# Four cross-attention layers on one core: interleaved opening, and a mask split into eight pieces

## The reference

```python
def bit_quant(W):
    gamma = jnp.mean(jnp.abs(W))
    Wq = jnp.clip(jnp.round(W / (gamma + Q_EPS)), -1.0, 1.0) * gamma
    return W + jax.lax.stop_gradient(Wq - W)
...
xn = layer_norm(x, ln_gamma, ln_beta)
q = xn @ bit_quant(Wq).T + bq
k = context @ bit_quant(Wk).T + bk
v = context @ bit_quant(Wv).T + bv
```

```python
scores = jnp.einsum('bhqd,bhkd->bhqk', q, k) / math.sqrt(HD)
scores = scores + attention_mask
```

## Time and profile before

| | us |
|---|---|
| median of 3 runs | 585.86 |
| lowest, highest | 583.68, 589.11 |
| the profiled execution | 585.07 |
| its span, first to last instruction | 583.3 |

### The profile page before, as it was taken

One profiled execution on the slowest core, in us unless ns is written; L12 is line 12 of the kernel. 1 busy time (PEld: TensorE's weight loads), 2 busy tenths in 40 slices (PEclk: granted clock), 3 DMA queues, 4 the chain that ended last, 5 costly groups with the idle time before them and its releaser, 6 DMA issues.

```text
span 583.3 us, 14128 instructions
## 1 busy us (share of the span) xinstructions
PE 506.8 (87%) x5446; PEld 404.7 (69%) x5446; DVE 404.7 (69%) x1005; ACT 316.9 (54%) x761; POOL 251.8 (43%) x281
## 2 busy tenths in 40 slices
PE   0699999879999996895669699899999999998985
PEld 0367887657777775784547477788787878776874
DVE  4368866788777775256487979787878987784522
ACT  1177887647777776475242636455564636344331
POOL 4645633478788787889310313132222223112110
PEclk9999999989999999999678999999999999999998
DMA  9920000000000000000000000000000000000000
GB/s 295 269 111 3 2 3 3 2 3 1 3 4 2 3 3 1 1 1 2 0 1 0 2 1 0 1 1 11 2 10 1 1 11 1 9 2 10 1 10 18
DMA packets 12121, 11.75 MB, mean 20 GB/s; under 512 B 5144, under 2 KB 10136, under 8 KB 11928
## 3 DMA queue, kind: packets, MB, share of 16 engines
q1 hardware_dynamic: 11624, 9.54, 5.9%
q10 hardware_dynamic: 432, 1.32, 0.6%
HBM read 9.81 MB, written 1.05 MB: 19 GB/s over the span
## 4 chain that ended last, share of the span: by engine, by line
PE 51%; DVE 26%; issue 10%; POOL 7%; ACT 5%; DMA 1%; POOLq 0%; DVEq 0%; ACTq 0%
PE ps L436 7%; DVE wide L1225 5%; PE ps L450 4%; PE ps L426 4%; PE ps L418 4%; PE ps L574 4%; DVE wide L1230 3%; PE ps L588 3%; PE ps L610 3%; DVE mx L1286 2%; PE ps L664 2%; PE ps L379 2%; DVE p L1288 2%; PE ps L461 2%; PE ps L380 2%
## 5 line engine op out<-in xcount | busy, mean ns | idle before, releaser
L1446 POOL TENSOR_TENSOR probs<-p,rc 128x512 f32<-128x512 f32 x32 | 33.7, 1054 | 155.9 <-DVE rc L1297 155.9
L1057 DVE TENSOR_REDUCE negm<-ps 128x8 bf16<-128x512 f32 x96 | 59.6, 682 | 24.8 <-PE ps L418 24.8
L911 ACT ACTIVATE p<-p 128x512 f32<-128x512 f32 x32 | 20.2, 631 | 101.2 <-DVE p L1288 101.2
L574 PE MATMUL ps<-shared,wq 128*128 128x256 f32 x256 | 68.7, 396 | 4.6 <-DVE w L1256 2.3
L765 ACT ACTIVATE shared<-ps 128x512 f32<-128x512 f32 x96 | 57.4, 600 | 24.3 <-PE ps L436 22.6
L1408 POOL TENSOR_TENSOR wide<-wide,cv 128x1024 f32<-128x1024 f32 x24 | 49.3, 2053 | 48.4 <-DVE wide L1036 48.4
L1353 POOL TENSOR_TENSOR rstd<-veps,neghalf 128x2 f32<-128x2 f32 x40 | 29.1, 728 | 74.6 <-DVE veps L1081 47.5
L1225 DVE TENSOR_TENSOR wide<-ps,cst 128x512 f32<-128x512 f32 x64 | 43.2, 675 | 25.4 <-PE ps L574 25.4
L436 PE MATMUL ps<-cst,p 128*128 128x128 f32 x384 | 59.2, 278 | 0.4 <-ACT shared L765 0.4
L759 ACT ACTIVATE p<-ps 128x512 f32<-128x512 f32 x96 | 54.5, 596 | 7.4 <-PE ps L426 7.3
L574 PEld LDWEIGHTS ps<-shared,wq 128*128 128x128 f32 x256 | 46.6, 195 | 15.5 <-DVE w L1256 4.3
(11 more groups left out here) (180 smaller groups left out, 1173.3 us busy)
## 6 DMA issues: line engine op xcount, KB each, us to landing
late<-in_mask_l SPq DMA_DIRECT2D x2, 512.0 KB, 8.7
wq<-in_wq SPq DMA_DIRECT2D x1, 1024.0 KB, 8.6
result<-x_all SPq DMA_DIRECT2D x8, 128.0 KB, 1.8
x_all<-in_x_tok SPq DMA_DIRECT2D x1, 896.0 KB, 9.9
wide<-in_ctx_t SPq DMA_DIRECT2D x1, 896.0 KB, 11.6
rv<-in_rv ACTq DMA_DIRECT2D x1, 768.0 KB, 7.4
cst<-in_cst ACTq DMA_DIRECT2D x1, 512.0 KB, 4.8
wa<-in_wa SPq DMA_DIRECT2D x1, 512.0 KB, 9.5
```

The costliest lines, as they stand in the source:

```text
L574: ins = mm(bank_of(f"q{i}", g)[:, j * GT:j * GT + GT], wq3[:, 2 * i + j, :], hn_t[:, g % 2, 0:GT], start=True, stop=True, skip_group_check ...
L1057: V.tensor_reduce(negm[:, n % 4, :], ps[:, S_BANK[r], :].rearrange("p (a k) -> p a k", k=S), AX.X, ALU.max, negate=True).then_inc(sm["dve_ ...
```

## The change

In the opening, group 1 gets PSUM bank N for its input, q, k and v, so it needn't wait for v of group 0. The four matrices are quantised one by one, each with a semaphore count of its own; q and k need two, v three, and the output projection all four. The fourth is quantised in pass 0, behind two evacuations of v. Normalising group 1 moves from POOL to DVE (norm0). The first loads of x and of the context bring two groups. ACT first loads only the identity (64 KB) and the columns of biases, and issues the rest of its loads when the first part of the context is there; it casts the other selectors in pass 4. The mask is split in eight pieces of 256 columns in passes 10 to 17, all five operations of a piece in one pass.

```diff
-        A, N, PV = ps[:, A_BANK, :], ps[:, N_BANK, :], ps[:, PV_BANK, :]
+        N, PV = ps[:, N_BANK, :], ps[:, PV_BANK, :]
+
+        def a_bank(w):
+            return ps[:, N_BANK if w == 1 else A_BANK, :]
...
-            eng.dma_start(x_all[:, 0:TG, :], x_v[:, 0:TG, :]).then_inc(sm["ld_x0"], 16)
-            eng.dma_start(ctx_t[:, 0:GT], dr["ctx_t"][:, 0:GT]).then_inc(sm["ld_ctx0"], 16)
-            eng.dma_start(x_all[:, TG:NT, :], x_v[:, TG:NT, :]).then_inc(sm["ld_x"], 16)
-            eng.dma_start(ctx_t[:, GT:], dr["ctx_t"][:, GT:]).then_inc(sm["ld_ctx"], 16)
+            eng.dma_start(x_all[:, 0:2 * TG, :], x_v[:, 0:2 * TG, :]).then_inc(sm["ld_x0"], 16)
+            eng.dma_start(ctx_t[:, 0:2 * GT], dr["ctx_t"][:, 0:2 * GT]).then_inc(sm["ld_ctx0"], 16)
+            eng.dma_start(x_all[:, 2 * TG:NT, :], x_v[:, 2 * TG:NT, :]).then_inc(sm["ld_x"], 16)
+            eng.dma_start(ctx_t[:, 2 * GT:], dr["ctx_t"][:, 2 * GT:]).then_inc(sm["ld_ctx"], 16)
...
-                if w >= 1:
-                    pe.wait_ge(sm["dve_v"], w)
+                if w >= 2:
+                    pe.wait_ge(sm["dve_v"], 1 if w == 2 else w)
...
                 if w == 0:
-                    pe.wait_ge(sm["quant"], 1)
+                    pe.wait_ge(sm["quant"], 2)
...
             def project_v(w):
                 ph = w // NG
                 pe.wait_ge(sm["act_q"], w + 1)
+                if w == 0:
+                    pe.wait_ge(sm["quant"], 3)
...
             def project_out(w):
                 pe.wait_ge(sm["act_at"], w + 1)
+                if w == 0:
+                    pe.wait_ge(sm["quant"], 4)
...
             transposes_in(0)
             project_qk(0)
-            project_v(0)
             transposes_in(1)
             project_qk(1)
+            project_v(0)
...
-            pe.wait_ge(sm["m3_split"], 1)
+            pe.wait_ge(sm["m3_split"], 5 * (B // 4))
...
-            act.dma_start(cst[:, :], dr["cst"]).then_inc(sm["ld_small"], 16)
+            act.dma_start(cst[:, 0:128], dr["cst"][:, 0:128]).then_inc(sm["ld_small"], 16)
             act.dma_start(cv[:, :], dr["cv"]).then_inc(sm["ld_small"], 16)
+            act.wait_ge(sm["ld_small"], 32)
+            A_(idb[:, 0, :], cst[:, 0:128], ACT.Copy).then_inc(sm["cst_bf"], 1)
+            act.wait_ge(sm["ld_ctx0"], 16)
             act.dma_start(rv[:, :, :].rearrange("p a b -> p (a b)"), dr["rv"].partition_broadcast(128))\
                .then_inc(sm["ld_rv"], 16)
-            act.wait_ge(sm["ld_small"], 32)
-            A_(idb[:, :, :].rearrange("p a b -> p (a b)"), cst[:, 0:128 * NSEL], ACT.Copy).then_inc(sm["cst_bf"], 1)
+            act.dma_start(cst[:, 128:], dr["cst"][:, 128:]).then_inc(sm["ld_cst"], 16)
+
+            def cast_selectors():
+                act.wait_ge(sm["ld_cst"], 16)
+                A_(idb[:, 1:, :].rearrange("p a b -> p (a b)"), cst[:, 128:128 * NSEL], ACT.Copy).then_inc(sm["cst_bf"], 1)
...
             for w in range(NW + 2):
+                if w == 4:
+                    cast_selectors()
...
+            def quantise(i):
+                c = slice(i * 128, i * 128 + 128)
+                pos, neg, w = probs_t[:, 0, c], probs_t[:, 1, c], wa[:, 0, i, :]
+                V.tensor_scalar(pos, w, qg[:, 2, i:i + 1], qg[:, 0, i:i + 1], ALU.is_gt, ALU.mult)
+                V.tensor_scalar(neg, w, qg[:, 3, i:i + 1], qg[:, 0, i:i + 1], ALU.is_lt, ALU.mult).then_inc(sm["q_gc"], 1)
+                dve.wait_ge(sm["q_gc"], 3 * i + 1)
+                V.tensor_tensor(pos, pos, neg, ALU.subtract).then_inc(sm["q_gc"], 1)
+                dve.wait_ge(sm["q_gc"], 3 * i + 2)
+                V.tensor_tensor(pos, pos, w, ALU.subtract).then_inc(sm["q_gc"], 1)
+                dve.wait_ge(sm["q_gc"], 3 * i + 3)
+                V.tensor_tensor(w, w, pos, ALU.add).then_inc(sm["quant"], 1)
+
+            def norm0(g):
+                dve.wait_ge(sm["ln0_r"], g + 1)
+                for t in range(TG):
+                    ins = V.tensor_scalar(xn_all[:, TG * g + t, :], x_all[:, TG * g + t, :], mv[:, g % 2, t, 0:1],
+                                          rstd[:, g % 2, t:t + 1], ALU.subtract, ALU.mult)
+                ins.then_inc(sm["ln0"], 1)
...
-                if step == 0:
+                b = slice(4 * c, 4 * c + 4)
+                n = 5 * c
+                if c == 0:
                     dve.wait_ge(sm["ld_w3"], LD_W3)
-                    V.tensor_copy(m3a[:, :, :], m3[:, :, :]).then_inc(sm["m3_split"], 1)
-                    dve.wait_ge(sm["m3_split"], 1)
-                    V.tensor_tensor(m3[:, :, :], m3[:, :, :], m3a[:, :, :], ALU.subtract).then_inc(sm["m3_split"], 1)
-                elif step == 1:
-                    dve.wait_ge(sm["m3_split"], 2)
-                    V.tensor_copy(m3b[:, :, :], m3[:, :, :]).then_inc(sm["m3_split"], 1)
-                    dve.wait_ge(sm["m3_split"], 3)
-                    V.tensor_copy(m3a[S:128, :, :], m3b[S:128, :, :]).then_inc(sm["m3_split"], 1)
-                elif step == 2:
-                    dve.wait_ge(sm["m3_split"], 4)
-                    V.tensor_tensor(m3b[:, :, :], m3[:, :, :], m3b[:, :, :], ALU.subtract).then_inc(sm["m3_split"], 1)
+                V.tensor_copy(m3a[:, b, :], m3[:, b, :]).then_inc(sm["m3_split"], 1)
+                dve.wait_ge(sm["m3_split"], n + 1)
+                V.tensor_tensor(m3[:, b, :], m3[:, b, :], m3a[:, b, :], ALU.subtract).then_inc(sm["m3_split"], 1)
+                dve.wait_ge(sm["m3_split"], n + 2)
+                V.tensor_copy(m3b[:, b, :], m3[:, b, :]).then_inc(sm["m3_split"], 1)
+                dve.wait_ge(sm["m3_split"], n + 3)
+                V.tensor_copy(m3a[S:128, b, :], m3b[S:128, b, :]).then_inc(sm["m3_split"], 1)
+                dve.wait_ge(sm["m3_split"], n + 4)
+                V.tensor_tensor(m3b[:, b, :], m3[:, b, :], m3b[:, b, :], ALU.subtract).then_inc(sm["m3_split"], 1)
...
             ln0(0)
+            scales()
+            quantise(0)
+            quantise(1)
             ln0(1)
+            quantise(2)
+            norm0(1)
             dve.wait_ge(sm["ld_small"], 32)
             evac_k(0)
-            evac_v(0)
+            evac_k(1)
             ln0(2)
-            evac_k(1)
...
+                if w == 0:
+                    evac_v(0)
                 if w + 1 < NW:
                     evac_v(w + 1)
+                if w == 0:
+                    quantise(3)
...
-                if w >= NG + 2:
+                if 0 <= w - NG - 2 < B // 4:
                     split_mask(w - NG - 2)
...
             def ln0_r(g):
                 pool.wait_ge(sm["ln0_ve"], g + 1)
                 rsqrt(rstd[:, g % 2, :], veps[:, g % 2, :], TG, sm["ln0_r"])
+                if g == 1:
+                    return
...
             mask_k(0)
+            mask_k(1)
             ln0_r(2)
-            mask_k(1)
```

More of the change, by code:

```diff
@@ L372, in project_qk @@
                 if w == 0:
-                    pe.wait_ge(sm["quant"], 1)
+                    pe.wait_ge(sm["quant"], 2)
                     pe.wait_ge(sm["ld_ctx0"], 16)
-                elif w == 1:
+                elif w == 2:
                     pe.wait_ge(sm["ld_ctx"], 16)
@@ L378, in project_qk @@
                     pe.wait_ge(sm["ld_wa"], 16)
-                mm(A[:, 0:GT], wa[:, ph, 0, :], in_t[:, w % 2, :], start=True, stop=True)
-                mm(A[:, GT:2 * GT], wa[:, ph, 1, :], kv_src(w), start=True, stop=True).then_inc(sm["pe_qk"], 1)
+                mm(a_bank(w)[:, 0:GT], wa[:, ph, 0, :], in_t[:, w % 2, :], start=True, stop=True)
+                mm(a_bank(w)[:, GT:2 * GT], wa[:, ph, 1, :], kv_src(w), start=True, stop=True).then_inc(sm["pe_qk"], 1)
             def project_v(w):
@@ L400, in scores @@
                     pe.wait_ge(sm["m_bias"], 1)
+                    pe.wait_ge(sm["cst_bf"], 2)
                 rows = [slice(32 * r, 32 * r + 32) for r in range(RG)]
@@ L441, in weigh_values @@
                 pe.wait_ge(sm["act_pt"], RG * (w + 1))
-                pe.wait_ge(sm["dve_v"], w + 1)
+                pe.wait_ge(sm["dve_v"], max(w + 1, 2))
                 if w >= 2:
@@ L742, in evac_in @@
                 if ph == 0:
-                    ins = A_(in_t[:, w % 2, :], A[:, 0:GT], ACT.Identity, bias=col("b0"), scale=col("g0"))
+                    ins = A_(in_t[:, w % 2, :], a_bank(w)[:, 0:GT], ACT.Identity, bias=col("b0"), scale=col("g0"))
                 else:
-                    ins = A_(in_t[:, w % 2, :], A[:, 0:GT], ACT.Copy)
+                    ins = A_(in_t[:, w % 2, :], a_bank(w)[:, 0:GT], ACT.Copy)
                 ins.then_inc(sm["act_in"], 1)
@@ L751, in evac_q @@
                     act.wait_ge(sm["pe_s"], w - 1)
-                A_(q_t[:, w % 2, :], A[:, 0:GT], ACT.Identity, bias=col(f"bq{w // NG}")).then_inc(sm["act_q"], 1)
+                A_(q_t[:, w % 2, :], a_bank(w)[:, 0:GT], ACT.Identity, bias=col(f"bq{w // NG}")).then_inc(sm["act_q"], 1)
             def exps(w, r):
@@ L991, in _ @@
             dve.wait_ge(sm["q_sum"], 1)
```

(19 more changed lines are left out.)

10 lines of the change are left out of this document (5 added, 5 removed).

## The result

| | before | changed |
|---|---|---|
| median of 9 runs, us | 586.29 | 591.61 |
| lowest, highest | 583.68, 589.11 | 587.47, 593.52 |
| profiled execution, its span | 585.07, 583.3 | 589.09, 586.9 |

The ratio is 1.0078 with a 95% interval of 1.0051 to 1.0106: 4.6 us slower (the two medians lie 5.3 us apart). The forecast was 588.0.

What follows compares the result with a forecast made beforehand. It took TensorE to bound the attention passes and a serial latency chain the opening. From the profiled 585.07 us, -6.1 for the opening and +9.0 for the split gave 588.0 us, range 582.5 to 594.0.

Steps and rivals of the forecast that it cites:

- The split: Eight mask pieces in passes 10 to 17, taking turns with POOL: 9.0 us more than the old split.
- The first maximum behind a piece: On DVE after a piece: starts 3.70 us from the cast's start, instead of 1.67 if alone.
- Second operation: A piece's first tensor_tensor on DVE, waiting for POOL's multiplication: 2.0 us for its own 0.43.
- Passes of 10.03: Length of an attention pass with a piece, from pass 11 on; the first takes 10.15 us.
- the second rival: Pieces held longer, POOL's power keeping DVE out to its end: 1.05 us more in 8 passes, 596.4 us; chance 0.12.
- The opening: Start of the kernel: first maximum at 20.8 for 27.52, 6.7 us earlier; net of what is given back -6.1 us.
- DVE gets the sum at 6.70, as now: Start of the opening's chain on DVE: the sum's time unchanged; possibly up to half a us earlier, counted at nothing.
- Given back: Part of the opening's gain lost later: 0.45 us from pass 0, 0.15 from casting the selectors on ACT in pass 4.
- a rival of 0.08 with 6 us: Clock falls in half of the passes with pieces, as PE waits about 1.5 us in each: 594; chance 0.08.
- the two terms of the forecast: Over the whole kernel: -6.1 us from the opening and +9.0 us from the split.
- the pieces are hidden: In the passes with pieces: their 1.67 us fit the room of 1.67, so the split costs nothing: 572.0; chance 0.08.
- The half opening: The opening brings half only, through a late load or POOL's scaling beside the first two matrices: 591; chance 0.10.

Runs made afterwards that it cites:

- e2: The kernel before with only the eight mask pieces changed, its old opening kept: 596.26 us, ratio 1.016 to the kernel before.
- e3: The changed kernel with one more wait on POOL, holding its mask multiplication until the piece's five operations are done: 575.19 us, ratio 0.9793 to the kernel before.
- e4: The changed kernel with the split as one large operation in each of passes 10 to 16: 573.79 us, ratio 0.9771 to before; timed again 573.09 us.

## Why the prediction was right, and where it was off

**The split: right in each step.** The own duration of the cast was summed wrongly: 0.16 and an eighth of 1.06 are 0.29, not 0.28, and it measured 0.28. The first maximum behind a piece at 3.70 from the cast: 3.71. Second operation 2.03 to its end: 2.02. Second cast: 0.70 both ways. Passes of 10.03: 10.03. Pass 10 to 18 80.3 us: 80.37 in e2, and 81.82 less one fall of 1.45 in the profile after. e3 shows that POOL is the cause. POOL's power does not keep DVE out to its end: the copy took 0.22 just behind its start. With that the second rival (596.4) is out. The Trainium skill, "SBUF — State Buffer", section "Who interferes with whom", says that whoever issues first holds the pair of ports shared by DVE and GpSimd for the whole instruction. By that, the trace agrees for POOL's multiplication (2.02 for 0.42 us on DVE), and differs for its power (0.22 us beside it).

**The opening: mis-sized.** The step "DVE gets the sum at 6.70, as now" failed. The weights landed 1.1 us earlier (4.14 for 5.27), outside the half a us that I had allowed. The forecast spoke of them as on ACT's queue; they come by SyncE's, and the 512 KB went beside them. Counted from the sum the forecast was 15.53 and the run 15.45. That is partly luck: the scores started 13.34 us behind the sum and not 13.83, and the maximum came 2.11 us behind them and not 1.72, as the score matmuls took 2.01 us for 1.59. (The forecast's terms for a matrix add up to 1.58, not 1.56, and so matrices 0 and 1 end at 11.6 and not 11.4.) Given back were 0.6 instead of 0.45 in passes 0 and 1, and nothing instead of 0.15 in pass 4. Net -7.35 for -6.1.

**The clock: taken too lightly.** I gave it a rival of 0.08 with 6 us. PE's waits are 1.6 to 1.85 us, not 1.5. The length of a wait alone doesn't decide: the fall came at a wait of 1.82 us (169.64), and none at those of 1.82 (159.62) and 1.85 (181.13). The profiled run has one fall in the eight passes, 1.45 us, and 0.5 us in the tail. With the opening that makes 585.07 - 7.35 + 10.56 - 0.10 + 0.5 = 588.7 against 589.09 measured. The median is 2.5 us above the profiled run, whose mean clock is 0.970; six of the other eight have a lower one. The one changed run at 0.977 took 587.47, runs of before at 0.977 take 584.7 to 585.1; at 0.968 it is 591.4 to 592.0 and 589.1 to 589.3. At an equal mean clock the change costs 2.1 to 2.9 us, and the two terms of the forecast give 2.9. The rest, some 2 us of the 4.6, goes with the clock. That 588.0 came within 1.1 us of the profiled 589.09 is luck in part: the opening brought 1.25 us more than forecast, and the falls of the clock took 2 us that the sum had at nothing. (The lower end of the range does not come out of its terms: 3.2 for the turns, 0.6 for the loads and 0.5 for the copy lead to 583.7 and not 582.5. The result lies near the upper end.)

**The other rivals.** That the pieces are hidden needs POOL out of the way: e3 and e4 are that case, at 575.2 and 573.8, where 572.0 was worked out. In the profile of e4 (573.5) the passes gave back the 6.9, the opening brought 1.5 us more than forecast, and the tail was 2.9 us longer than before the change. In that of e3 the passes from 10 to 18 are 1.9 us longer than in e4, and so is the tail. The half opening did not come.

## What to carry to other kernels

Before work of DVE is put into its idle time, look what POOL does in that time. If POOL runs a tensor_tensor on SBUF, then a tensor_tensor or a cast of DVE on SBUF takes turns with it, and each short operation of a dependent chain can wait for a whole operation of the other. Cut such work by operation and not by column: one large operation per pass, begun just ahead of POOL's, pays once or never. And look at the loads that are issued beside the first one: when they changed here, its landing moved by 1 us.

## What the runs showed of the hardware

Whoever comes first decides: a half subtraction (1.21 us) begun 0.17 us ahead of POOL's 1.89 us multiplication made it 2.80 in e4 and was not stretched itself, and a piece's subtraction begun behind it took 2.02 for 0.42 us. A cast is held as a subtraction is (0.70 for 0.28 us, behind POOL's residual). POOL's power is the exception: two DVE operations ran unstretched beside it. A layer norm's scalar operation on 128 x 2 elements is held as well, which the forecast of the opening did not have: with POOL's multiplication beside it, it took 1.35 us instead of 0.17.

```profile
17.86 1.35 DVE L1018 TENSOR_SCALAR veps<-mv 128x2 f32<-128x2 f32 x1
```

And the low clock is worth as much as the change: with an equal list of instructions the tail was 367.5 to 375.9 us, and a single fall in it cost 2.5 us.
